# Counting edges into blocks: ScalarE zeroes the PSUM banks, TensorE reads one word for two steps

## What is computed

```python
for l in range(n_layers):
    agg = jax.ops.segment_sum(h[src], dst, num_segments=n) / deg
    h = jax.nn.relu(agg @ W_agg[l] + h @ W_self[l] + b_hid[l])
```

## Time and profile before

| | us |
|---|---|
| median of 3 runs | 7610.15 |
| lowest and highest | 7608.11, 7611.19 |
| the profiled execution, its own time | 7667.53 |
| its span, first to last instruction | 7665.8 |
| the build, from the first L1498 to the first L1352 | 903.4 |

### The profile page before, as it was taken

One profiled execution on the slowest core, in us unless ns is written; L12 is line 12 of the kernel. 1 busy time (PEld: TensorE's weight loads), 2 busy tenths in 40 slices (PEclk: granted clock), 3 DMA queues, 4 the chain that ended last, 5 costly groups with the idle time before them and its releaser, 6 DMA issues.

```text
span 7665.8 us, 108469 instructions
## 1 busy us (share of the span) xinstructions
PE 6321.0 (82%) x29032; PEld 4993.3 (65%) x29033; DVE 3412.8 (45%) x9453; ACT 1651.3 (22%) x4349; POOL 2239.8 (29%) x2541
## 2 busy tenths in 40 slices
PE   5877799999999999766676765999999966777677
PEld 3555477778887777655555554777787755555555
DVE  7766666661111222355555566122233324444443
ACT  1344410000000111111111113132233332222222
POOL 1000010001001111366666652000111116666664
PEclk8887799999999999878877887999999988878887
DMA  4566777788779777533333336988977753333332
GB/s 138 181 228 242 256 284 261 256 299 312 273 277 343 262 257 256 184 83 83 85 82 84 83 90 200 333 291 294 354 249 244 243 181 97 102 100 99 100 100 75
DMA packets 606869, 1525.79 MB, mean 199 GB/s; under 512 B 72808, under 2 KB 248915, under 8 KB 606612
## 3 DMA queue, kind: packets, MB, share of 16 engines
q1 hardware_dynamic: 472803, 1129.19, 41.8%
q0 software_dynamic: 133824, 393.46, 17.0%
HBM read 1206.47 MB, written 316.80 MB: 199 GB/s over the span
## 4 chain that ended last, share of the span: by engine, by line
PE 59%; DVE 11%; another core or an unknown queue 11%; issue 8%; DMA 6%; DVEq 2%; ACT 2%; SPq 1%; POOL 0%; ACTq 0%; POOLq 0%
PE psum L1352 33%; PE psum L1498 4%; PE psum L1198 4%; PE psum L1646 3%; PE psum L1618 2%; PE psum L1549 2%; DMA slab<-adj 2%; DVE hot_j L2309 2%; DVE acc L2547 2%; DMA g_own<-own_dram 2%; PE psum L1630 1%; PE psum L1537 1%; PE psum L1193 1%; PE psum L1286 1%
## 5 line engine op out<-in xcount | busy, mean ns | idle before, releaser
L1352 PE MATMUL psum<-X,slab 128*128 128x512 f32 x12495 | 3111.2, 402 | 74.9 <-DMA slab<-adj 41.3
L1352 PEld LDWEIGHTS psum<-X,slab 128*128 128x128 f32 x12495 | 2347.7, 191 | 608.5 <-DVE g_x L2374 89.7
L2547 DVE TENSOR_TENSOR acc<-acc,psum 128x264 f32 (+1 forms) x1660 | 702.8, 423 | 1068.8 <-PE psum L1646 353.0
L1498 PE MATMUL psum<-hot_j,hot_key 128*128 128x392 bf16 x1592 | 570.9, 431 | 164.2 <-DVE hot_j L2309 109.4
L1012 POOL DMA_DIRECT2D table<-s_tab x147 | 80.4, 547 | 1910.8 <-DVE s_tab L2065 1910.8
L1537 PE MATMUL psum<-node_tabs,onehot_t 128*128 x1660 | 274.7, 305 | 378.3 <-ACT onehot_t L1822 348.2
L1537 PEld LDWEIGHTS psum<-node_tabs,onehot_t 128*128 128x128 f32 x1660 | 274.0, 248 | 420.6 <-issue 414.3
L1102 POOL DMA_INDIRECT ring<-gat_table,idx_slot x420 | 415.7, 990 | 261.2 <-ACT idx_slot L1817 138.1
L1102 POOL DMA_INDIRECT ring<-rel_table,idx_slot x420 | 412.6, 982 | 250.2 <-ACT idx_slot L1817 137.7
L1723 ACT CAST staged<-psum 128x392 fp32r<-128x392 f32 x808 | 373.0, 489 | 522.3 <-PE psum L1498 497.0
L1498 PEld LDWEIGHTS psum<-hot_j,hot_key 128*128 128x128 bf16 x1592 | 235.7, 148 | 321.7 <-issue 236.2
(11 more groups left out here) (426 smaller groups left out, 8124.2 us busy)
## 6 DMA issues: line engine op xcount, KB each, us to landing
slab<-adj SPq DMA_DIRECT2D x383, 1344.0 KB, 6.7
slab<-adj SPq DMA_DIRECT2D x313, 896.0 KB, 6.2
adj<-staged SPq DMA_DIRECT2D x808, 196.0 KB, 1.9
X<-table SPq DMA_DIRECT2D x32, 1792.0 KB, 13.4
table<-s_tab POOLq DMA_DIRECT2D x196, 256.0 KB, 3.5
g_own<-own_dram POOLq DMA_DIRECT2D x35, 896.0 KB, 8.1
own_dram<-s_out POOLq DMA_DIRECT2D x196, 128.0 KB, 5.1
acc<-zero_rows SPq DMA_DIRECT2D x2, 6600.0 KB, 27.4
```

The source lines that it names most:

```text
L1352: last = nc.tensor.matmul(sums_of(j), slab[:, slab_at(c), u, j * P:(j + 1) * P], X[:, x_at(p, d), :], start=(d == 0), stop=(d == KT - 1))
L1498: nc.tensor.matmul(psum[:, bass.ds(own, 1), 0:J].rearrange("p o j -> p (o j)"), hot_key[:, s % KEYS // AT_ONCE, :, s % AT_ONCE], hot_j[:, ...
L2547: V.tensor_tensor(a, a, psum[:, bank, 0:w], ALU.add).then_inc(sem("summed"), 1)
```

## The change

The number of banks stays four. What changes:

- ScalarE writes zeros (`zero_j`, 128x392, 32 bit) into a bank after it has copied it: after the copy of part r it zeroes the bank of part r-1. These zeroings now count up `evicted`, four of them ahead of the first part; the copies count up a new semaphore, `taken`, for which SyncE waits.
- TensorE has no product of two columns any more. It waits for `evicted` ahead of a step's product, not behind it.
- VectorE adds, once, the part numbers of steps 2k and 2k+1 into one word (`pair_part`). Since the second number is the first or one more, both follow from the sum. TensorE loads 16 such words at step 0 of a turn, and none at step 16. The part number of the next step is worked out ahead of this step's product.

```diff
-    LEAD = RING - 1
+    LEAD = RING
...
-            def cleared(bank_ap):
-
-                nc.tensor.matmul(bank_ap, iota_k[:], iota_k[:, 0:2], start=True, stop=True, skip_group_check=True)
+            def part_of(s):
+
+                return pe.snap((pe.snap(zs[s // 2]) + s % 2) // 2, min_val=1, max_val=LEAD + ENDED)
 
             def build(t, steps):
                 for s in range(steps):
                     beside(in_stages, t, s)
-                    if s % NOW == 0:
-                        pe.load(zs, step_part[0:1, bass.ds(t * BUILD + s, NOW)])
-                    z = pe.snap(zs[s % NOW], min_val=1, max_val=LEAD + ENDED)
+                    if s == 0:
+                        pe.load(zs, pair_part[0:1, bass.ds(t * NOW, NOW)])
+                        z = part_of(s)
                     if s % 4 == 0:
                         pe.wait_ge(*ev("hot", t * BUILD + (s + 4)))
+                    pe.wait_ge(sem("evicted"), z)
                     own = (z % RING).with_bounds(min_val=0, max_val=RING - 1)
+                    if s + 1 < steps:
+                        z = part_of(s + 1)
                     nc.tensor.matmul(psum[:, bass.ds(own, 1), 0:J].rearrange("p o j -> p (o j)"), hot_key[:, s % KEYS // AT_ONCE, :, s % AT_ONCE], hot_j[:, s % HOT, :],
                                      start=False, stop=True, skip_group_check=True).then_inc(sem("meet_mm"), 1)
-                    pe.wait_ge(sem("evicted"), z)
-                    next_own = ((z + 1) % RING).with_bounds(min_val=0, max_val=RING - 1)
-                    cleared(psum[:, bass.ds(next_own, 1), J:J + 2].rearrange("p o j -> p (o j)"))
...
+            def zeroed(bank):
+
+                nc.scalar.copy(psum[:, bank, 0:J], zero_j[:]).then_inc(sem("evicted"), 1)
+
...
-                    nc.scalar.copy(staged[:, r, :], psum[:, (r + 1) % RING, 0:J]).then_inc(sem("evicted"), 1)
-
+                    nc.scalar.copy(staged[:, r, :], psum[:, (r + 1) % RING, 0:J]).then_inc(sem("taken"), 1)
+                    if not (isinstance(i, int) and r == 0):
+                        act.wait_ge(*ev("taken", i * AT_ONCE + r))
+                        zeroed(r % RING)
+
+            act.wait_ge(*ev("zero_j", 1))
+            for z in range(1, RING + 1):
+                zeroed(z % RING)
...
+            V.memset(zero_j[:], 0.0).then_inc(sem("zero_j"), 1)
             dve.wait_ge(*ev("rec_stored", 16))
             dve.wait_ge(*ev("step_part", 16))
             dve.wait_ge(*ev("parts_stored", 16 * SB2))
-            V.tensor_copy(iota_k[:], iota_row[:])
+            of_pair = step_part.rearrange("p (n two) -> p n two", two=2)
+            once(V.tensor_copy(pair_tmp, of_pair[:, :, 1]))
+            V.tensor_tensor(pair_part, of_pair[:, :, 0], pair_tmp, ALU.add).then_inc(sem("pair_part"), 1)
```

More of the change, by code:

```diff
@@ L87, in build @@
     assert BTURNS == T + 1 and SB2 * P - MEETS + ENDED + MORE < ELSEWHERE
+    PAIRS = SB2 * P // 2
+    assert MEETS % 2 == 0 and BTURNS * NOW <= PAIRS
     KT = PARTS * DG // P
@@ L205, in build @@
             at_now = COLS + 2 * T
-            iota_k = node_tabs[:, at_now:at_now + P // 2].bitcast(BF16)
             edge_now = node_tabs[:, at_now + P // 2:at_now + P // 2 + BUILD]
@@ L212, in build @@
             step_part = g_x[0:1].rearrange("p j d -> p (j d)")[:, 0:SB2 * P].bitcast(I32)
+            pair_part, pair_tmp = (g_own[0:1].rearrange("p j d -> p (j d)")[:, n * PAIRS:(n + 1) * PAIRS].bitcast(I32) for n in range(2))
             iota_j = sb("iota_j", [P, J], BF16, scope=scope)
@@ L278, in build @@
                 staged = sb("staged", [P, AT_ONCE, J], F32R, scope=late)
+                zero_j = sb("zero_j", [P, J], scope=late)
         with ExitStack() as scope:
@@ L505, in build @@
                              ("cuts", 1), ("bound_read", 1), ("cuts_read", 1), ("z_rows", 1), ("parts_out", 1), ("marks", 1), ("x_ve", 1), ("more_rows", 1),
-                             ("b_self", 1), ("rows2_f", 2), ("x_rstd", 1), ("chunk_i", 1), ("edge_f", 2), ("turn_row", 1), ("w_att", 2 * Q),
+                             ("b_self", 1), ("rows2_f", 2), ("x_rstd", 1), ("chunk_i", 1), ("zero_j", 1), ("pair_part", 1), ("edge_f", 2), ("turn_row", 1), ("w_att", 2 * Q),
                              ("amax", 1), ("gdiag", 1), ("dst_tab", 1), ("zs_clamped", 1), ("bn_ve", 1), ("bn_shift", 1),
@@ L729, in parts_out @@
                 for r in range(AT_ONCE):
-                    sp.wait_ge(*ev("evicted", i * AT_ONCE + (LEAD + r + 1)))
+                    sp.wait_ge(*ev("taken", i * AT_ONCE + (r + 1)))
                     to = sp.snap(to_regs[r], min_val=0, max_val=PARTS + MORE - 1)
@@ L1506, in _ @@
             pe.wait_ge(*ev("rows2_T_read", 2 * NR))
-            pe.wait_ge(*ev("step_part", 16))
-            pe.wait_ge(*ev("hot", 1))
-            cleared(psum[:, 1, J:J + 2])
+            pe.wait_ge(*ev("pair_part", 1))
             by_meets(pe, build, 2)
+            pe.wait_ge(*ev("taken", ENDED))
             pe.wait_ge(*ev("evicted", LEAD + ENDED))
@@ L1728, in _ @@
                 parts_evicted(i)
+            act.wait_ge(*ev("taken", ENDED))
+            zeroed(ENDED % RING)
             act.wait_ge(*ev("steps_T", 1))
@@ L2107, in _ @@
             V.memset(carrier[:, 5:6], 0.0).then_inc(sem("summed"), GB)
-            V.memset(carrier[:, 7:8], 0.0).then_inc(sem("evicted"), LEAD)
             dve.wait_ge(*ev("iota", 6))
```

## The result

The changed kernel takes 7572.0 us in the median (7564.1 to 7583.8) against 7611.2 us for the kernel before in the same comparison (7608.1 to 7621.9): a ratio of 0.9951, 95% interval 0.9937 to 0.9964, 39 us less. The forecast was 7543 us, 67 less than its 7610: the direction came out, and 39 of the 67 us. The profiled execution took 7574.1 us (span 7572.4). That of before had 7667.5 us.

The account below looks back on a forecast made before the run. TensorE's queue was taken to bound the build's first stretch, ScalarE the other two after the change. -49 - 12 - 8 + 2 = -67 us, from 7610 to 7543 us; own range 7514 to 7592 (chance 0.58), wide range 7483 to 7640.

Parts of the forecast that it names:

- The first stretch: Build's first 15 turns: step-16 load and second product leave TensorE's queue; 13.5 us a turn, 202 us, 49 less.
- Rival D: TensorE's steps get no quicker: one-hot waits uncovered, register work eats the second product; within 15 us of 7610; chance 0.10.
- ScalarE's pair: ScalarE's queue: a copy and a zeroing together take 0.82 us; with 0.11 for the load, 0.93 us a part.
- Rival B: ScalarE's pairs do not overlap in the second and third stretch: 1.15 us a part, 66 us more, 7676; chance 0.13.
- Rival A: ScalarE overlaps fully and queues mesh: 0.86 us a part, no coupling loss, early turns 12.6 us; 7467 us; chance 0.12.
- I add 0.5 us a turn, 7 and 10 us: Second and third stretch: four banks couple TensorE and ScalarE, which can lack work; 7 and 10 us added.
- 5 us for slots: Third stretch: waits for written slots, 17.2 us before the change, stay in part; 5 us added.
- the second stretch: Build's next 14 turns, 245 parts, bound by ScalarE at 0.93 us a part: 235 us, 12 less.
- the third: Build's last 21 turns, 410 parts, bound by ScalarE at 0.93 us a part: 397 us, 8 less.
- ScalarE is done first: End of the build: the last 20 steps add no part, so ScalarE finishes first; nothing added.
- Rival C: TensorE's array stays at the low clock: 23 us more in the first stretch, covered by ScalarE elsewhere; 7566; chance 0.07.
- SyncE and the two more operations of VectorE: SyncE's wait for `taken` costs nothing; VectorE's operations ahead of the build, about 1 us each, add 2 us.

Follow-up runs that it names:

- two_loads: packed with TensorE's register load as before the change, sixteen step numbers at steps 0 and 16, ScalarE still zeroing; ratio 1.0022 to the kernel before.
- second_product: packed plus a second product of two unread columns per step on TensorE, without register work of its own; ratio 1.0112 to the kernel before.
- one_wait: packed with TensorE waiting once per pair of steps, for the odd step's part, three register operations per pair instead of five; ratio 0.9983 to the kernel before.
- wide_zero: packed with ScalarE zeroing all 512 columns of a bank instead of 392; ratio 1.0041 to the kernel before.
- narrow_zero: packed with ScalarE zeroing only 8 columns of a bank, so its sums are wrong; ratio 0.9894 to the kernel before.
- packed: The changed kernel with two 16-bit part numbers side by side in a word instead of their sum, ScalarE's wait numbers masked; ratio 0.998 to the kernel before.
- one_wait_last: one_wait together with ScalarE's last-step numbers packed as in packed_last; ratio 0.9948 to the kernel before.
- packed_last: packed with ScalarE's last-step numbers packed too, a load of four words for eight parts instead of eight; ratio 0.9953 to the kernel before.
- cleared_masked: The kernel before with a mask on each part number in TensorE's queue; ratio 1.0334 to the kernel before.

## Why the prediction was right, and where it was not

**The sign and its reason.** Both pieces that it took off TensorE's queue were there, and their removal is the gain. The first stretch came out at 198.9 us for a forecast of 202. Steps 0.32 us apart for 0.33, no gap at step 16, a turn of 13.3 us for 13.5: as put. *two_loads*, *second_product* and *one_wait* each moved one thing in TensorE's queue, the load, a small product and register work, and the first stretch followed each time. Rival D falls with that.

**ScalarE's pair** had no row of its own and was taken as 0.82 us; it is 0.80. Rival B (1.15) is out. Rival A had the better price for a part, 0.86 against 0.93 where 0.84 came out (below), but not its second half, that nothing is lost between the engines. The page "ScalarE: Activation LUTs" of the Trainium skill, section "What ACT_TABLE_LOAD costs", comes out well for the zeroing (by its figures an estimate of 0.513 us for one and 0.42 in a row, in the trace 0.511 in the median and 0.42) and high for the copy out (0.38 in a row).

**The step that failed is "I add 0.5 us a turn, 7 and 10 us", with the 5 us for slots.** Behind 298.8 us there are 655 parts in 651 us. Their pairs take 655 x 0.80 = 524 us, which leaves 127. Four things share it. The last part is done at 940.3 us and the build ends at 949.9, which is 10 us. The waits for TensorE are 86.2 us and for slots 12.7, and each wait costs 0.1 us more than its idle time, for the copy behind it then stands 0.52 us behind the zeroing, the idle time not counted, and not 0.42. The loads of the part numbers stand inside these waits: the first copy of eight, which needs the load, begins 0.88 us behind the zeroing in the median, the seven others 0.42. In the mean it is 1.03 against 0.54 us, 81 x 0.49 = 40 us more; 12 of these are slots, and the other 28, 0.35 us each, I put down to the loads.

The forecast had 0.93 x 655 = 609 us of work and 22 of waiting; it was 524 + 28 = 552 and 99. So ScalarE's own price was put 57 us too high, and its waiting 77 us too low. That the first error hid most of the second was luck. 20 us stayed: 4 in the second stretch and 16 in the third, which had the wrong sign. 10 of these 16 are the end behind the last part, which the forecast put at nothing ("ScalarE is done first") though it priced the stretch by ScalarE alone; before the change it was 13 us.

The wider reason: two engines with four banks between them did not run at the pace of the slower one. Each waits for the other now and then (76.8 and 86.2 us), and the later stretches answered to both: longer with dearer work on TensorE (*two_loads*, *second_product*) or on ScalarE (*wide_zero*), shorter by 30% of the saving with cheaper work on ScalarE (*narrow_zero*). That parts of uneven length are behind these waits is argued; no run changed the lengths or the number of banks.

**The clock.** Rival C said it would stay low in the first stretch; it rose from 0.85 to 0.97. The Trainium skill's page "TensorE: Matmul & The Clock Gate", section "A second HAM failure mode: psum-queue depth-cycling", tells of a kernel that cycled through banks and lost throughput by small gaps; the first stretch here does not agree, with four banks in turn and 0.97 granted. The third looks more like it: the clock, which C had called covered by ScalarE there, fell from 0.76 to 0.66, with TensorE now waiting for zeroed banks, 180 times behind the first stretch. With a cheap zeroing it was 0.79 (*packed*: 0.67), and the stretch 36 us shorter. Behind the first stretch steps in a row are 0.34 us apart in the median at the low clock and 0.305 at the full one, so a step costs more there; how much of that reaches the time, and whether the clock or the waits come first, no run here separates.

**SyncE and the two more operations of VectorE:** nothing to see in the rows; the build began 0.7 us earlier, not 2 later.

**From the profile to the medians.** "Nothing ties that difference to the build" was mostly so: the rest took 39 us less in the profile after. Of the 28 us by which the median missed the forecast, 13 are the terms above (16 + 4 too little, 4 + 3 too much), and 15 are the difference between the profiles' 54 us and the medians' 39, which is open.

No version ran that is clearly faster than the changed kernel and computes all: *one_wait_last* and *packed_last* are level with it, although both start from *packed* (0.998 against 0.9951). By these ratios the changed kernel with packed last-step numbers would stand near 0.9951 - 0.0027 = 0.992. This is an estimate; it was not run.

## What to carry to other kernels

Before moving work from a waiting engine to an idle one, do not only compare the two prices: count the buffers between the two. If both end up near the same pace with few buffers, book the waiting of each for the other as a term of its own (here 0.14 us per part on 0.84 of work), and count the end, where the slower engine has nothing left to do, by itself. And where products wait on values from registers, count the register pieces in the queue: the first stretch lost 53 of 252 us when one load a turn and, in each step, one small product with its register work went.

## What the runs showed of the hardware

- Register operations in TensorE's queue can cost more than they last: two pieces of 29 and 32 ns, most steps' addition in *cleared_masked*, made a step 0.17 us longer, 0.56 against 0.384 at the same clock. The gain can be smaller: two pieces less per pair of steps gave 14 us over 240 pairs, 0.03 us each (*one_wait*), with VectorE busy for 177 of the 192 us.
- A register load takes time by the word: 306 and 539 ns at least for 4 and 8 words on ScalarE, 1105 for 16 on TensorE, some 67 ns a word.
- Behind a standstill of some 2 us at the load TensorE ran at 1.2 GHz (0.50 from 174 to 178 us before the change), and with the load gone that stood there, the clock of the stretch was 0.97. *two_loads* put the load back and had 0.85, the value of before.
- The same ScalarE copy follows its predecessor after 0.38 us where it needs nothing of it, and after 0.51 us where it waits for its end.

The row for the second point, TensorE's load of 16 words after the change; those of 8 and 4 stand at *packed_last*.

```profile
L1496 PEldq TENSOR_LOAD <-g_own x50: 1105/1379/2817, 96.8 to 940.6; - x50
```
